# Self-attention scores as six 64-row products in two row tiles instead of four 128-row products

## What is computed

```python
q = (xq @ wq).reshape(B, S, N_HEADS, D_HEAD)      # B=2, S=1024, 16 heads of 64
k = (xkv @ wk).reshape(B, T, N_HEADS, D_HEAD)     # T=S here
attn = jnp.einsum('bihd,bjhd->bhij', q, k) * scale
attn = jax.nn.softmax(attn, axis=-1)
out = jnp.einsum('bhij,bjhd->bihd', attn, v).reshape(B, S, D_ATTN)
```

## Time and profile before

| what | value |
|---|---|
| median of 3 runs | 1049.37 us (1048.73 to 1055.62) |
| the profiled execution | 1052.94 us |
| its span, first to last instruction | 1051.2 us |
| TensorE clock granted, mean share | 0.995 |
| main loop, first to last row maximum | 32.4 to 770.7 us |
| PE busy, share of the span | 95% |
| DVE busy, share of the span | 81% |
| ACT busy, share of the span | 59% |

### The profile page before, as it was taken

How to read it: one execution, slowest core, us unless ns; L and a number is a source line. 1 busy time by engine, 2 the same in 40 slices (tenths; PEclk the granted TensorE clock), 3 DMA queues, 4 the chain that set the end, 5 groups by cost and what they waited for, 6 DMA issues and landing times.

```text
span 1051.2 us, 28671 instructions
## 1 busy us (share of the span) xinstructions
PE 1003.5 (95%) x12258; PEld 796.1 (76%) x12258; DVE 852.4 (81%) x996; ACT 624.0 (59%) x1152; POOL 299.0 (28%) x268
## 2 busy tenths in 40 slices
PE   8999999999989999999999999998999999999998
PEld 6777777777767778777777777665777888888887
DVE  4688999999999878999998899998868898554433
ACT  4756666676666665676666676665755545443322
POOL 5113222333322123433223233211314346701000
PEclk9999999999999999999999999999999999999999
DMA  8896676587566766666775775696210001100000
GB/s 180 228 232 157 143 159 145 127 166 156 123 145 126 169 137 137 141 151 134 151 161 127 145 157 108 144 226 125 47 62 21 2 11 41 51 1 21 21 5 37
DMA packets 179647, 121.39 MB, mean 115 GB/s; under 512 B 142656, under 2 KB 159552, under 8 KB 175040
## 3 DMA queue, kind: packets, MB, share of 16 engines
q1 hardware_dynamic: 179520, 119.55, 51.6%
HBM read 56.60 MB, written 12.58 MB: 66 GB/s over the span
## 4 chain that ended last, share of the span: by engine, by line
PE 55%; issue 22%; DVE 9%; POOL 7%; ACT 4%; SPq 3%; DMA 1%; DVEq 0%; POOLq 0%; ACTq 0%
PE W L639 13%; PE SC L612 12%; PE SC L717 8%; PE W L585 5%; PE W L727 4%; POOL X L479 4%; DVE nmax L1210 4%; PE W L895 3%; PE W L595 3%; SPq L263 3%; PE SC L705 2%; PE W L652 1%; DVE PR L1215 1%; DMA w_raw<-in_L_xattn_sa_wk_dram 1%; PE W L882 1%
## 5 line engine op out<-in xcount | busy, mean ns | idle before, releaser
L975 ACT ACTIVATE PR<-SC,nmax 128x1024 f32<-128x1024 f32 x256 | 287.1, 1122 | 214.2 <-DVE nmax L1210 213.9
L1210 DVE TENSOR_REDUCE nmax<-SC 128x1 f32<-128x1024 f32 x256 | 304.6, 1204 | 36.7 <-PE SC L612 36.2
L1215 DVE STREAM_TRANSPOSE PR<-PR 128x1024 f32<-128x1024 f32 x256 | 314.5, 1234 | 12.5 <-ACT PR L975 1.4
L612 PE MATMUL SC<-QKS 128*128 128x512 f32 x1024 | 287.6, 411 | 21.7 <-ACT PR L975 21.4
L479 POOL TENSOR_TENSOR X<-f_raw,X 128x512 f32<-128x512 f32 x128 | 163.0, 1290 | 461.0 <-ACT f_raw L1002 461.0
L612 PEld LDWEIGHTS SC<-QKS 128*128 128x128 f32 x1024 | 180.1, 188 | 100.5 <-ACT PR L975 50.7
L639 PE MATMUL W<-PR,V 32*64 32x256 f32 x8192 | 242.1, 380 | 1.3 <-issue 1.3
L639 PEld LDWEIGHTS W<-PR,V 32*64 32x64 f32 x8192 | 185.7, 132 | 51.9 <-issue 18.4
L1002 ACT ACTIVATE f_raw<-W,rden 128x256 f32<-128x256 f32 x256 | 101.4, 477 | 0.5 <-POOL X L479 0.3
L1283 DVE SCALAR_TENSOR_TENSOR GU<-SC,b,GU 128x512 f32<-128x512 f32 x32 | 24.0, 750 | 69.3 <-ACT GU L1038 69.3
L1038 ACT ACTIVATE GU<-SC,b 128x512 f32<-128x512 f32 x32 | 22.1, 690 | 85.1 <-PE SC L717 85.1
(11 more groups left out here) (132 smaller groups left out, 1485.9 us busy)
## 6 DMA issues: line engine op xcount, KB each, us to landing
QKS<-QKT SPq DMA_DIRECT2D x64, 512.0 KB, 6.4
V<-scratch_v SPq DMA_DIRECT2D x128, 256.0 KB, 4.9
QKS<-QKT SPq DMA_DIRECT2D x128, 128.0 KB, 4.5
scratch_v<-VST SPq DMA_DIRECT2D x32, 256.0 KB, 4.5
wo<-in_L_xattn_sa_wo_dram SPq DMA_DIRECT2D x64, 64.0 KB, 3.0
f_raw<-in_L_xattn_ff_w_dram SPq DMA_DIRECT2D x12, 256.0 KB, 3.1
X<-in_x_dram SPq DMA_DIRECT2D x4, 512.0 KB, 5.3
w_raw<-in_L_xattn_sa_wk_dram SPq DMA_DIRECT2D x16, 128.0 KB, 3.5
```

Source lines behind the costliest of these rows:

```text
L612: last = mm(SC[t % 2][:, cols], QKS[:, 3 * s, t * P:(t + 1) * P], QKS[:, 3 * s + 1 + l, cols], start=(l == 0), stop=(l == 1))
L975: nc.scalar.activation(PR[:, NT * s + t, :], SC[t % 2][:, :], ACT.Exp, bias=nmax[:, t % 4:t % 4 + 1], accum_out=den[:, s, t:t + 1]).then_i ...
L1210: V.tensor_reduce(nmax[:, t % 4:t % 4 + 1], SC[t % 2][:, :], AX, ALU.max, negate=True).then_inc(d_max, 1)
L1215: V.transpose(tile, tile).then_inc(d_tr, 1)
```

## The change

`place` now puts q high in both halves of the partitions, and q low in both (two 1024-wide rows), and the keys once: k high and k low of keys 0 to 511 in partitions 0 to 63 and those of keys 512 to 1023 in partitions 64 to 127, side by side in one row. `scores` makes three terms for each half of the keys. Each is a product over 64 rows, and the two halves alternate, so that consecutive matmuls lie in different row tiles and write different banks. A tile signals s_sc twice, and the waits count accordingly. The number of DMAs of a placement, six, stays; the keys go in two of 256 KB (by the profile's count of bytes read and written) instead of two of 512 KB, the queries in four of 256 KB instead of four of 128 KB.

```diff
@@ place
-                move(QKS[0:64, 3 * h + 1:3 * h + 3, :], QKT[r, 2:4, :], m_qk[h])
-                move(QKS[64:128, 3 * h + 1:3 * h + 3, :], QKT[r, 2:4, :], m_qk[h])
-                for half, signal in enumerate((m_qk[h], m_q1[h])):
-                    cols = slice(half * BANK, (half + 1) * BANK)
-                    move(QKS[0:64, 3 * h, cols], QKT[r, 0, cols], signal)
-                    move(QKS[64:128, 3 * h, cols], QKT[r, 1, cols], signal)
+                halves = [slice(0, BANK), slice(BANK, 2 * BANK)]
+                sides = [slice(0, 64), slice(64, P)]
+                for side, keys in zip(sides, halves):
+                    move(QKS[side, 3 * h + 2, :].rearrange("p (a n) -> p a n", a=2), QKT[r, 2:4, keys], m_qk[h])
+                for signal, cols in zip((m_qk[h], m_q1[h]), halves):
+                    for side in sides:
+                        move(QKS[side, 3 * h:3 * h + 2, cols], QKT[r, 0:2, cols], signal)
@@ SyncE
-                    sp.wait_ge(s_sc, NT * h)
+                    sp.wait_ge(s_sc, 2 * NT * h)
...
-                    sp.wait_ge(s_sc, NT * (h + 1))
+                    sp.wait_ge(s_sc, 2 * NT * (h + 1))
@@ scores
-                for half in range(2):
-                    cols = slice(half * BANK, (half + 1) * BANK)
-                    for l in range(2):
-                        last = mm(SC[t % 2][:, cols], QKS[:, 3 * s, t * P:(t + 1) * P], QKS[:, 3 * s + 1 + l, cols],
-                                  start=(l == 0), stop=(l == 1))
-                last.then_inc(s_sc, 1)
+                for c, (l, r) in enumerate(TERMS):
+                    for half in range(2):
+                        rows, cols = slice(64 * half, 64 * half + 64), slice(half * BANK, (half + 1) * BANK)
+                        last = mm(SC[t % 2][:, cols], QKS[rows, 3 * s + l, t * P:(t + 1) * P],
+                                  QKS[rows, 3 * s + 2, r * BANK:(r + 1) * BANK], start=(c == 0), stop=(c == 2))
+                        if c == 2:
+                            last.then_inc(s_sc, 1)
@@ rowmax
-                dve.wait_ge(s_sc, N + 1)
+                dve.wait_ge(s_sc, 2 * N + 2)
```

## The result

| | kernel before | after the change |
|---|---|---|
| median, 20 runs each | 1049.51 us (1047.12 to 1058.65) | 1047.78 us (1044.91 to 1051.30) |
| ratio, 95% interval | 1 | 0.9965 [0.9949, 0.9980], 3.7 us |
| the profiled execution | 1052.94 us | 1047.77 us |
| start, to the first row maximum | 32.4 us | 31.6 us |
| main loop | 738.3 us | 734.1 us |

The change gains, as forecast, less than the 1% that a measurement tells from no change in three runs; in twenty runs the gain is seen: 3.7 us by the ratio (the two medians alone differ by 1.7), where 8.3 were forecast. Between the groups it was mostly the kernel before that moved: its median was 1049.5 us here and 1053.7, 1055.1 and 1055.6 beside the experiments, that of the kernel after 1047.8 here and 1046.6 there.

A forecast was written before the change was run, and what follows sets the result against it. A loop through PE's scores and bursts, the add and the exponential bounds the kernel, PE gains capped by DVE's idle before the add. 17 x 0.46 + 0.5 = 8.3 us gives 1041.5 us; range 1033 to 1057.

The forecast's parts named there:

- The pairs: In the scores, two 64-row matmuls run side by side in 0.23 us; a tile takes 0.70 us, 0.23 less.
- the upper bound of 0.46: Largest time in us allowed for a pair of 64-row score matmuls: two alone, one after another.
- the rival in which they don't overlap: Score matmuls of a pair run one after another: each tile 1.4 us, kernel 1180 us; chance 0.04.
- The switch: Each change of PE's tiling between scores, projections and bursts costs about 0.195 us, half going out, half going in.
- the forecast's own terms, -1.16, +0.78 and -0.07: Loop to the end of burst two: five lighter tiles, four new switches, V's entry already paid; together -0.46 us.
- six tiles 7, 0, 1: Score tiles with a 128-row filler behind, needing two switches each; ten switches per ordinary head instead of six.
- DVE is late next: The add of the halves can come forward 0.48 us; behind it DVE has no gap left.
- The count of heads: 17 places gain 0.46 us each, two 0.5 together: 8.3 us; heads behind `PLAIN` about 0, head 0 loses 0 to 0.5.
- what hides the rest: Placement DMAs in 2 KB pieces, the doubled signal and 1024 more instructions in PE's queue cost 0 each.
- nothing can be measured: Rival: DVE is nearly full and part of its gaps moves to another wait; 1048 to 1049 us, chance 0.16.
- A dearer switch or pair: Rival: PE becomes the bound through fillers around tiles 7, 0 and 1; at twice the switch cost 1080 us; chance 0.10.
- Nearly free switches: Rival: tiling switches hide; 17 places reach their caps, seven PE-bound heads gain up to 1.86 us each; 1030 us, chance 0.15.

The follow-up runs named there:

- e3: Kernel after the change with scores in 128-row tiles, three matmuls in place of six (scores differ), no tiling switches between scores and fillers: 1036.36 us, 0.9835.
- e5: Kernel after the change with 128 already-met waits put into PE's start-up: 1048.72 us, 0.9947.
- e9: Kernel before the change with 128 already-met waits put into PE's start-up: 1056.13 us, one run.
- e13: Kernel before the change with 28 already-met waits in PE's start-up: 1057.28 us, one run.
- e16: Kernel after the change with 56 already-met waits in PE's start-up: 1043.41 us, one run.
- e7: Kernel after the change with score loops swapped, three matmuls of one half, then three of the other: 1048.09 us, one run.
- e15: Kernel after the change with 28 already-met waits in PE's start-up: 1045.60 us, one run.
- e2: Kernel after the change, unchanged, run for a second profile: 1049.58 us, one run.
- e8: Kernel after the change, unchanged, timed again in a second group of runs: 1046.63 us, 0.9928.
- e10: Kernel after the change with three score matmuls of one half, then three of the other, each on its own line: 1048.04 us, one run.

## Why the prediction was right, and where not

**The pairs**: right. Two 64-row matmuls of 512 columns in float32r start 3 to 10 ns apart, and the next two 0.23 us later: full rate, and neither the upper bound of 0.46 nor the rival in which they don't overlap.

**The switch**: right. In the profile of after, the first matmul behind a switch starts 0.09 us late and the second another 0.10, 0.19 in all where 0.195 was forecast; e3 gives 0.165 in a head that PE bounds. The loop got 0.37 shorter from its start to the end of burst two, and ordinary heads 0.41, where 0.46 were forecast (the forecast's own terms, -1.16, +0.78 and -0.07, give 0.45): the tile's gain and the switches cancel to a small rest, and 0.05 to 0.09 of it is the error of that. The forecast counts "six tiles 7, 0, 1"; they are three tiles with six switches, and its sum uses six switches, so nothing hangs on the slip.

**DVE is late next**: right. The idle before the add went down by 0.29, e3 with a PE that is faster still wins 0.04 per head, and PE's wait before the output projection grew.

**The count of heads**: right in the sum and wrong in the parts. 15 heads gave 6.2 us. Heads 2 and 16 gave 0.20 instead of 0.46 each: the first row maximum after the switch comes later there (DVE's idle before it went from 0.33 to 0.66) and eats half of it. Head 0, with fillers behind every tile, lost 0.68 where 0 to 0.5 stood. Heads 1, 12 and 15 lost 0.2 where 0 stood: in head 15 the lighter tiles alone, as e3 has them, gave 24.63 - 23.17 = 1.46 instead of the 1.86 of the forecast, and ten switches took 1.65 instead of 1.95. Against this stand heads 13, 29, 30 and 31, which gave 2.3 us that I had not counted. Together it is 8.5; that this is so near 8.3 is luck, since 2.3 us uncounted on one side make up for what the other parts missed.

**The failed step** is the last one of "what hides the rest": "1024 more matmul and weight-load instructions go through PE's queue; it kept up with 28 ns each in the bursts (3.64 / 128) ..., so 0". The rate at which the queue issues was right; what feeds it was left out. The program comes in blocks of 256 instructions, and at some of them PE waits, in the kernel before as after. Adding 1024 instructions moved all later boundaries. In the pair of profiles the excess grew from 6.0 to 10.3 us, which is the half of the gain that is missing from that pair; in the heads in which PE stood still it grew from 3.6 to 8.3. That the stops move with the place of the boundaries is shown by e5, e9 and e13 to e16. How much of the missing gain they explain in the *median* isn't settled: the timed gains were 3.7 and 7.6 us in two groups, whose intervals overlap, so between 4.6 and 0.7 us of the forecast are missing there, and it was the kernel before whose median moved between the groups, by 5.6 us, against 1.2 for the kernel after. Why the kernel before was so fast in the first group stays open. Why a block comes late at one boundary and in time at another isn't shown either. In the 2 us before the late transfers of after began (packets 8, 36, 38, 58 and 65) queue q1 alone held the DMA engines for 92 to 113% of the time, but so it was, by over 90%, before about half of all the packets in the loop, most of which made no stop; and the late transfers themselves took 0.9 to 1.5 us, like others. No run took the other traffic away.

**A second part of the excess** is the clock, though not of its growth. The kernel after in three stretches (us, busy us (x) of PE, PEld, DVE, ACT, POOL, granted clock, DMA share, GB/s), the first head 12, the second a part of it, the third head 15 for the earlier trace rows:

```profile
301.94:329.02 27.08, 23.23 (x337) 15.76 (x337) 24.05 (x30) 16.81 (x34) 6.21 (x6) 0.94 0.70 140
...
314.40:317.80 3.40, 3.40 (x80) 2.54 (x72) 3.40 (x6) 1.33 (x3) 0.00 (x0) 0.50 0.40 96
...
379.82:404.65 24.83, 24.36 (x357) 17.72 (x358) 20.10 (x19) 15.47 (x30) 9.14 (x10) 1.00 0.46 109
```

The clock is 0.50, the level of 1.2 GHz, for 3.4 us of head 12. PE had waited just before, as the timeline of after shows:

```profile
313.13 0.96 PE L616 MATMUL SC<-QKS 64*128 64x512 f32 x6 [2.00 <-ACT PR L980]
314.02 5.40 PE L644 MATMUL W<-PR,V 32*64 32x256 f32 x128
```

The same place in e5:

```profile
315.26 0.96 PE L616 MATMUL SC<-QKS 64*128 64x512 f32 x6 [1.43 <-ACT PR L982]
316.15 3.71 PE L644 MATMUL W<-PR,V 32*64 32x256 f32 x128
```

Head 12 takes 27.08 us in after and 25.61 in e5. The wait alone doesn't bring the clock down, though. The same place in e7:

```profile
313.25 0.98 PE L616 MATMUL SC<-QKS 64*128 64x512 f32 x6 [2.02 <-ACT PR L980]
314.16 3.71 PE L644 MATMUL W<-PR,V 32*64 32x256 f32 x128
```

In e7, e15 and e16 PE waited 1.40 and then about 2.0 us as in after, the burst took its 3.71 us, and head 12 took 26.1 to 26.2. So some 0.9 us are the clock's and 0.5 to 0.6 the longer wait's; what made the clock fall in after, e2, e8 and e10 and not in those three stays open. It also fell right behind the stops of 3.77 us in e3 and of 3.2 us in e13. The kernel before has no such stretch in head 12 but two near 704 and 728 us, in its heads 29 and 30, which lie 2.1 us over their shortest. So in the pair of profiles the clock took no more from after than from before.

**The rivals.** That nothing can be measured falls with the interval below 1, if only just. Its number, 1048 to 1049, lies nearer to the measured 1047.8 than the forecast's 1041.5; its mechanism, gaps that move to another wait, isn't what was seen, since the ordinary heads did gain 0.41 us each. A dearer switch or pair falls with 0.19 and 0.23. Nearly free switches, at 1030, is what e3 imitates: 17 us below the kernel before, where the rival said 20.

**The rest.** The placement of 2 KB pieces showed no wait on any operand in QKS; the doubled signal shows nowhere either. The loop starts at 30.9 to 31.6 us after and 31.6 to 32.4 before: no later, and if anything 0.7 us earlier, where the forecast said 0.

## What to carry to other kernels

Count the switches of tiling before packing rows: at 0.17 to 0.2 us each they ate more than half of what a quarter less matmul time in the scores would have brought here (e3 gained 17 us, the change 3.7 to 7.6), and putting two fillers of one tiling side by side brought another 0.45%. Measure an edit of a per cent or less over more than one place of the instruction stream, and in more than one group of runs: in single profiles some dozens of idle waits at the start, which cost nothing, went with loops 5 us shorter or 6 us longer, and the unchanged kernel before moved by 6 us between groups. And look for stops with the releaser "issue" in the middle of a burst; if two executions stop at the same instruction, and the stop moves when idle waits are put in front, the program is what is waited for. The same stop can bear another engine's name where it falls on a wait that is met.

## What the hardware did that I had not expected

- PE stands still at block boundaries of its own program, up to 1.5 us at a time in after, over 3 us in e13 (head 1, its 930th instruction) and 3.77 in e3; all excess together, the clock's share with it, was 4 to 14 us in a loop of 730. The transfer of a late block began 5 to 20 us after that of the one before it, and the engine went on 1.3 to 1.8 us behind its landing.
- PE starts a matmul of a free row tile ahead of waiting ones of another row tile that stand before it in the program (251 of 256 tiles in e10). The Trainium skill ("TensorE: Matmul & The Clock Gate", Part 3) says that matmuls start in program order without reordering; here the trace disagrees, and the interleaving written out by hand in the change was not needed.
- A switch of tiling shows in two places: the first matmul behind it starts 0.09 us late, and the second another 0.10.
- 128 waits that are met already cost 2.4 us on PE, 28 and 56 of them nothing that the start shows (30.8 to 32.0 us). 28 waits move a block boundary by 14 matmuls and weight loads, 56 by 28.
